# A sixth gate/up product ahead of the router's gate, transposes two products further back, and layer 2's queries copied ahead of weight casts

## What is computed

```python
logits = flat @ router_w.T
scores = jnp.sqrt(jax.nn.softplus(logits))
_, idx = jax.lax.top_k(scores + expert_bias, K)          # K = 4 of E = 32
topv = jnp.take_along_axis(scores, idx, axis=1)
topv = topv / (topv.sum(axis=-1, keepdims=True) + 1e-20)
probs = zeros.at[arange(T)[:, None], idx].set(topv)
def _clamped_swiglu(x, wg, wu, wd):                      # I = 128, ALPHA = 7
    return jax.nn.silu(jnp.clip(x @ wg.T, -ALPHA, ALPHA)) * jnp.clip(x @ wu.T, -ALPHA, ALPHA) @ wd.T
out = sum over the experts of probs[:, e:e+1] * _clamped_swiglu(flat, ...) + _clamped_swiglu(flat, shared ...)
```

## Time and profile before

| | before |
|---|---|
| median of 3 runs | 72.9 us (72.02 to 74.19) |
| profiled execution | 72.22 us |
| its span in the trace | 70.4 us |
| PE busy | 65.3 us, 93% |
| DVE busy | 47.0 us, 67% |
| ACT busy | 46.0 us, 65% |
| POOL busy | 54.2 us, 77% |
| transfers | 15.75 MB, done by about 44 us |
| granted PE clock | full in all slices but the last |

### The profile page before, as it was taken

How to read it: one execution, slowest core, us unless ns; L and a number is a source line. 1 busy time by engine, 2 the same in 40 slices (tenths; PEclk the granted TensorE clock), 3 DMA queues, 4 the chain that set the end, 5 groups by cost and what they waited for, 6 DMA issues and landing times.

```text
span 70.4 us, 1578 instructions
## 1 busy us (share of the span) xinstructions
PE 65.3 (93%) x542; PEld 48.5 (69%) x542; DVE 47.0 (67%) x133; ACT 46.0 (65%) x101; POOL 54.2 (77%) x60
## 2 busy tenths in 40 slices
PE   5999989999799999999989999999999999999940
PEld 2348647789564496467666878888887888788820
DVE  0089488486497536499999945679955887697440
ACT  0606375876998654769979899999668851275220
POOL 7430003889999996998799999999999999999000
PEclk9999999999999999999999999999999999999999
DMA  0998999999999999999999995200000000000002
GB/s 3 271 297 245 329 425 404 291 328 419 417 419 403 393 401 407 396 383 388 393 407 400 391 372 201 76 0 0 0 9 0 0 0 0 0 0 0 0 0 74
DMA packets 6343, 15.75 MB, mean 224 GB/s; under 512 B 704, under 2 KB 1472, under 8 KB 6336
## 3 DMA queue, kind: packets, MB, share of 16 engines
q1 hardware_dynamic: 6048, 15.39, 59.2%
q10 hardware_dynamic: 288, 0.27, 1.1%
HBM read 15.52 MB, written 0.13 MB: 222 GB/s over the span
## 4 chain that ended last, share of the span: by engine, by line
PE 52%; DMA 16%; DVE 14%; SPq 7%; ACT 4%; issue 3%; DVEq 0%; ACTq 0%
DMA gu_raw<-moe_w_dram 16%; PE bP L591 16%; PE bY L624 7%; PE bY L613 6%; PE bXT L603 5%; SPq L275 4%; PE bE L591 4%; DVE gu_clip L964 4%; PE bY L626 3%; SPq L283 2%; DVE h L1018 2%; PE bP L419 2%; PE bXT L448 1%; PE bXT L641 1%; PE bY L444 1%
## 5 line engine op out<-in xcount | busy, mean ns | idle before, releaser
L349 POOL TENSOR_TENSOR gu_w<-gu_raw,gu_w 128x512 fp32r<-128x512 f32 x27 | 33.7, 1277 | 0.6 <-ACT gu_w L705 0.6
L591 PE MATMUL bP<-gu_w,xnT_parts 128*128 128x512 f32 x66 | 18.6, 417 | 0.0
L591 PEld LDWEIGHTS bP<-gu_w,xnT_parts 128*128 128x128 f32 x66 | 12.2, 188 | 2.9 <-issue 0.5
L1018 DVE SCALAR_TENSOR_TENSOR h<-gu_clip,gate,bP 128x128 f32<-128x128 f32 x26 | 7.8, 344 | 5.2 <-ACT bP L790 5.2
L964 DVE TENSOR_SCALAR gu_clip<-bP,clip_at 128x512 f32<-128x512 f32 x13 | 10.4, 806 | 1.1 <-PE bP L591 1.1
L355 POOL TENSOR_TENSOR gu_w<-dn_w,gu_w 128x512 fp32r<-128x512 f32 x8 | 10.1, 1285 | 0.0
L698 ACT ACTIVATE gu_w<-gu_raw 128x1024 fp32r<-128x1024 f32 x9 | 9.4, 1048 | 0.3 <-issue 0.3
L796 ACT ACTIVATE hT_parts<-bXT 128x256 fp32r<-128x256 f32 x11 | 4.2, 383 | 7.1 <-PE bXT L603 7.1
L705 ACT ACTIVATE gu_w<-gu_raw 128x512 fp32r<-128x512 f32 x10 | 6.1, 621 | 1.2 <-DMA gu_raw<-moe_w_dram 1.2
L603 PE MATMUL bXT<-consts_sb,h 128*128 128x128 f32 x33 | 6.5, 277 | 0.3 <-DVE h L1018 0.2
L790 ACT ACTIVATE bP<-gu_clip,rstd 128x256 f32<-128x256 f32 x13 | 6.1, 472 | 0.4 <-DVE gu_clip L964 0.4
(11 more groups left out here) (161 smaller groups left out, 124.8 us busy)
## 6 DMA issues: line engine op xcount, KB each, us to landing
gu_raw<-moe_w_dram SPq DMA_DIRECT2D x16, 512.0 KB, 9.6
dn_w<-moe_w_dram SPq DMA_DIRECT2D x16, 256.0 KB, 9.5
aw_sb<-attn_w_dram SPq DMA_DIRECT2D x2, 512.0 KB, 7.4
shared_sb<-shared_w_dram SPq DMA_DIRECT2D x1, 416.0 KB, 14.9
small_sb<-small_dram SPq DMA_DIRECT2D x1, 338.0 KB, 7.3
xwq_sb<-x_wq_dram SPq DMA_DIRECT2D x1, 256.0 KB, 3.5
lora_sb<-lora_dram SPq DMA_DIRECT2D x1, 256.0 KB, 4.7
ctx_sb<-ctx_kv_dram ACTq DMA_DIRECT2D x1, 192.0 KB, 3.2
```

The lines of the kernel that those rows point to most:

```text
L349: nc.gpsimd.tensor_tensor(gu_w[:, gu_slot(p), 1, cols], gu_raw[:, raw_slot(p), cols], gu_w[:, gu_slot(p), 0, cols], ALU.subtract).then_inc ...
L591: last = nc.tensor.matmul(bGU[n % 5][:, 0:GU], xnT_parts[:, a, k, :], gu_w[:, gu_slot(n - 1), w, k * GU:(k + 1) * GU], start=(k == 0 and a ...
L1018: last = nc.vector.scalar_tensor_tensor(h[:, n % 4, e], gu_clip[:, n % 4, e, 1, :], weight_e, bank[:, e * 2 * I:e * 2 * I + I], ALU.mult, ...
```

## The change

First, `gate_up(6)` gets a bank of its own, `bXT1` (called `bOnce`), and is put ahead of `transpose_h(0)`; `gate_up(7)` stands between transposes 0 and 1. From then on `gate_up(n + 6)` stands ahead of `transpose_h(n)` until the pairs run out at n = 10, where it was `gate_up(n + 4)` until n = 12. `gate_up(n)` now waits for `gate_h(n - 6)` up to n = 11, and for `gate_h(n - 5)` from 12 on, since `bXT1` is used for a product only once. Since `bXT1` is taken, transposes 0 to 6 all go to `bXT0`, and each waits for the reader of the one just before it; from 7 on they alternate again.

The router's scratch values move to `bXT0`. The silu of the shared expert is written into the bank of pair 1, so `silu_unit(0)` waits for `clip(1)` and `gate_h(0)` for `silu_unit(1)`. The copy of `leftover` moves from the end of the router's chain on DVE to a place behind `logits_n`, ahead of a wait for ACT.

Last, ACT copies query 0 ahead of the first half of raw pair 4 and query 1 ahead of its second half, and casts only half of pair 5 ahead of the softmax; the other half follows `copy_probsT(1)`.

The core of the diff:

```diff
+BANKS = 6
+LEADS = ()
+def ahead(n):
+    return min(n + BANKS - sum(n >= at for at in LEADS), PAIRS)
...
-        logits_n, den, inv_root = (bXT1[:, at:at + E] for at in (64, 128, 192))
-        score2, weight = (bXT1[:, at:at + E + 1] for at in (256, 320))
-        bHT = (bXT1, bXT0)
+        logits_n, den, inv_root = (bShared[:, at:at + E] for at in (288, 320, 352))
+        score2, weight = (bShared[:, at:at + E + 1] for at in (384, 448))
-        bGU = (bP[0][:, 0], bP[0][:, 1], bP[1][:, 0], bP[1][:, 1], bE)
+        bOnce = bXT1
+        def bGU(n):
+            if n == BANKS:
+                return bOnce
+            return (bP[0][:, 0], bP[0][:, 1], bP[1][:, 0], bP[1][:, 1], bE)[(n if n < BANKS else n - 1) % 5]
+        def bHT(n):
+            return bXT0 if n <= BANKS or n % 2 == 0 else bXT1
...
             def gate_up(n):
-                if n > 5:
-                    pe.wait_ge(h_ready, n - 4)
+                if n > BANKS:
+                    pe.wait_ge(h_ready, n - BANKS + (1 if n < 2 * BANKS else 2))
...
             def transpose_h(n, width=2):
                 pe.wait_ge(h_ready, n + 1)
-                if n >= 2:
-                    pe.wait_ge(hT_ready, n - 1)
-                if n - 2 > FIRST:
-                    pe.wait_ge(hT_low_ready, n - 2 - FIRST)
+                back = 1 if n <= BANKS else 2
+                if n >= back:
+                    pe.wait_ge(hT_ready, n - back + 1)
+                if n - back > FIRST:
+                    pe.wait_ge(hT_low_ready, n - back - FIRST)
...
-            for n in range(WHOLE + 1, 6):
+            for n in range(WHOLE + 1, BANKS + 1):
                 gate_up(n)
             transpose_h(0, width=1)
+            gate_up(BANKS + 1)
             transpose_h(1)
             for n in range(2, PAIRS + 1):
-                if n + 4 <= PAIRS:
-                    gate_up(n + 4)
+                if ahead(n) > ahead(n - 1):
+                    gate_up(ahead(n))
                 transpose_h(n)
...
             for c in range(DC):
-                gu_high_chunk(WHOLE + 2, c)
                 act.wait_ge(q_psum, DC + c + 1)
                 nc.scalar.activation(qT[:, 1, c], bP[c][:, 1, 0:T], ACT.Identity,
                                      bias=small_sb[:, BIASQ + c:BIASQ + c + 1]).then_inc(q_ready, 1)
-            gu_high(WHOLE + 3)
+                gu_high_chunk(WHOLE + 2, c)
+            gu_high_chunk(WHOLE + 3, 0)
             exp_half(1, 0)
...
             copy_probsT(1)
+            gu_high_chunk(WHOLE + 3, 1)
             gu_high(WHOLE + 4)
...
             def silu_unit(n):
-                act.wait_ge(clip_ready, n + 1)
+                act.wait_ge(clip_ready, max(n, 1) + 1)
...
             step(nc.vector.tensor_scalar(logits_n, bLogits, rstd[:, 2:3], None, ALU.mult))
+            dve.wait_ge(zeroed, 3)
+            step(nc.vector.tensor_copy(score2[:, E:E + 1], leftover[:]))
             dve.wait_ge(one_plus_ready, 1)
...
             step(nc.vector.tensor_tensor(inv_root, inv_root, softplus[:], ALU.mult))
-            dve.wait_ge(zeroed, 3)
-            step(nc.vector.tensor_copy(score2[:, E:E + 1], leftover[:]))
```

More of the change, by code:

```diff
@@ L590, in gate_up @@
                         for a, w in HI_LO:
-                            last = nc.tensor.matmul(bGU[n % 5][:, 0:GU], xnT_parts[:, a, k, :],
+                            last = nc.tensor.matmul(bGU(n)[:, 0:GU], xnT_parts[:, a, k, :],
                                                     gu_w[:, gu_slot(n - 1), w, k * GU:(k + 1) * GU],
@@ L597, in transpose_h @@
                 pe.wait_ge(h_ready, n + 1)
-                if n >= 2:
-                    pe.wait_ge(hT_ready, n - 1)
-                if n - 2 > FIRST:
-                    pe.wait_ge(hT_low_ready, n - 2 - FIRST)
+                back = 1 if n <= BANKS else 2
[3 more added lines that the diff above has]
+                    pe.wait_ge(hT_low_ready, n - back - FIRST)
                 for e in range(width):
-                    last = nc.tensor.transpose(bHT[n % 2][:, e * T:(e + 1) * T], h[:, n % 4, e, :], ident)
+                    last = nc.tensor.transpose(bHT(n)[:, e * T:(e + 1) * T], h[:, n % 4, e, :], ident)
                 last.then_inc(hT_psum, 1)
@@ L619, in down @@
                     if n == PAIRS:
-                        pe.wait_ge(h_ready, PAIRS)
+                        pe.wait_ge(h_ready, PAIRS + 1)
                     for e in range(2):
@@ L785, in silu_unit @@
             def silu_unit(n):
-                act.wait_ge(clip_ready, n + 1)
+                act.wait_ge(clip_ready, max(n, 1) + 1)
                 width = 2 if n else 1
-                bank = bGU[n % 5] if n else bShared
-                dst = bank[:, 0:width * 2 * I].rearrange("p (e w i) -> p e w i", e=width, w=2)[:, :, 0, :]
+                dst = bGU(max(n, 1))[:].rearrange("p (e w i) -> p e w i", e=2, w=2)
+                dst = dst[:, :, 0, :] if n else dst[:, 0:1, 1, :]
                 nc.scalar.activation(dst, gu_clip[:, n % 4, 0:width, 0, :], ACT.Silu, scale=rstd[:, 2:3]
@@ L795, in hT_unit @@
                 dst = hT[:, n % 3, 0:width] if n <= FIRST else hT_parts[:, n % 3, 0]
-                nc.scalar.activation(dst, bHT[n % 2][:, 0:width * T], ACT.Copy).then_inc(hT_ready, 1)
+                nc.scalar.activation(dst, bHT(n)[:, 0:width * T], ACT.Copy).then_inc(hT_ready, 1)
             def dn_high(i):
@@ L821, in _ @@
                 for i in range(UNITS, LAST):
-                    if dn_from(i) + 1 == n + 4:
+                    if ahead(n - 3) <= dn_from(i) < ahead(n - 2):
                         dn_high(i)
@@ L956, in clip @@
                 width = 2 if n else 1
-                bank = bGU[n % 5] if n else bShared
+                bank = bGU(n) if n else bShared
                 if n:
@@ L1010, in gate_h @@
             def gate_h(n):
-                dve.wait_ge(silu_ready, n + 1)
+                dve.wait_ge(silu_ready, max(n, 1) + 1)
                 if n >= 4:
                     dve.wait_ge(hT_psum, n - 3)
-                bank = bGU[n % 5] if n else bShared
+                bank = bGU(max(n, 1))
+                at = 0 if n else I
                 for e in range(2 if n else 1):
@@ L1018, in gate_h @@
                     last = nc.vector.scalar_tensor_tensor(h[:, n % 4, e], gu_clip[:, n % 4, e, 1, :], weight_e,
-                                                          bank[:, e * 2 * I:e * 2 * I + I], ALU.mult, ALU.mult)
+                                                          bank[:, at + e * 2 * I:at + e * 2 * I + I], ALU.mult, ALU.mult)
                 last.then_inc(h_ready, 1)
@@ L1030, in hT_low @@
                 dve.wait_ge(hT_ready, n + 1)
-                nc.vector.tensor_tensor(hT_parts[:, n % 3, 1], bHT[n % 2][:, 0:2 * T].rearrange("p (e t) -> p e t", e=2),
+                nc.vector.tensor_tensor(hT_parts[:, n % 3, 1], bHT(n)[:, 0:2 * T].rearrange("p (e t) -> p e t", e=2),
                                         hT_parts[:, n % 3, 0], ALU.subtract).then_inc(hT_low_ready, 1)
```

2 lines of the change are left out of this document (1 added, 1 removed).

## The result

The changed kernel took 73.6 us in the median of five runs (72.65 to 74.65), the kernel before 72.47 us in five (71.79 to 74.19). The ratio is 1.0134, with the interval 1.0082 to 1.0186: between 0.8 and 1.9% slower. The forecast was 0.6% faster by ratio (0.994), and 72.1 us with a range of 71.1 to 73.3, so the measured median lies outside it. A later comparison of the same two kernels, with 12 and 35 runs, gave 1.0034 (0.9988 to 1.008), which can't be told from no change. Ratios leave disturbed executions out, medians hold all of them.

What follows compares the result with a forecast made beforehand. PE, busy 93% of the span, was taken as the bound, so only its waits could go: 0.36 (queries) + 0.95 (gate) - 0.89 (tail) = 0.42 us saved, 71.80 on the profiled execution; forecast 72.1 us, range 71.1 to 73.3.

Steps and rivals of the forecast that it cites:

- The queries' 0.36 us: Layer 2's first scores: PE no longer waits for the query copy behind a cast on ACT; 0.36 us saved, bounds 0 to 0.36.
- The tail's loss: Transposes 13 and 14: PE waits for DVE's work on the last pairs; 0.89 us lost, bounds 0 to 1.9.
- the queries' 0.36 is lost: Rival: one gain fails, by a cast late for POOL, heads copied late, or first transposes waiting; 72.2 us, 13%.
- The gate: Between product 5 and transpose 2: products 6 and 7 moved forward end PE's standing still; 0.95 us saved, bounds 0.6 to 0.95.
- The scratch bank, the silus and the copy of `leftover`: Smaller edits around the router, gate and transposes 0 to 6: expected to change nothing unless ACT falls a whole step behind.
- product 16 never waited for POOL: Expected sign: POOL ends the last low part at 55.07, product 16 starts at about 57.0; no cost.
- DVE's steps that don't overlap: Rival in the tail: each DVE step costs 1.83 us instead of 1.57; 0.56 us slower, 72.78 us, 9%.
- The rival on the other side: The rival of DVE steps without overlap in the tail: 1.83 us each, 0.56 us slower in all, 9%.

Runs made afterwards that it cites:

- The gate's half alone: The changed kernel with layer 2's new order of query copies and casts undone, against the kernel before: ratio 1.0074 (1.0025 to 1.0122).
- LEADS = (7, 9): The changed kernel with no product put ahead of transposes 7 and 9, against the kernel before: ratio 0.9935 (0.989 to 0.9981).

## Why the prediction was wrong

Two terms of the sum failed. The queries' 0.36 us were counted whole, and the runs show about nothing in most executions, 0.15 at the middle over three pairs of kernels. The tail's loss was put at 0.89 us and measured 1.22. Of the 0.78 us between the forecast (0.42 saved) and the profiles without the query's wait (0.36 lost), these two make 0.69.

**The queries.** The failed step is "I take the whole 0.36". The wait was in the profile, the mechanism was right, and the changed kernel's scores have no wait. But what ended the wait was a query copy behind a cast that itself had waited 0.71 us for a transfer, and that part is there in few executions. Of five profiles with the old order of ACT one shows the whole wait, one 0.11 us, and three none, two of these with a late start of layer 2. Measured by itself the edit gave 1.0009 (0.9965 to 1.0053). The rival "the queries' 0.36 is lost" was there, with 13%, but for the wrong reasons: I looked for a new wait that takes the gain, not for whether the old wait is there in most executions. ACT's copy of the heads came as counted, at 24.56 with no idle time ahead of it, and cost nothing.

**The gate.** Right within a tenth: 0.95 counted, 0.86 found. The kernel with the queries' edit alone has its S at 17.18 and transpose 9 at 54.99; with the gate's edit as well S is at 17.21 and transpose 9 at 56.98, with two more products ahead of it. That is 54.99 + 2.82 + 0.03 - 56.98 = 0.86. The sum's 0.95 was reached by a slip: it went on from the start of transpose 0's row (35.10) with slot lengths and compared the result with a slot. Product 5's row, in the timeline of the kernel before, ends at 35.23:

```profile
33.67 1.56 PE L591 MATMUL bP<-gu_w,xnT_parts 128*128 128x512 f32 x6
```

From there the slots (0.11, 0.22, 1.41) lead to 36.97, which leaves 0.82 to transpose 2's slot at 37.79. The scratch bank, the silus and the copy of `leftover` cost nothing that the trace shows, and product 16 never waited for POOL.

**The tail.** The mechanism is right to the row: pair 12's hidden values 2.08 us behind transpose 9 (56.98, 59.06), steps of 1.57 us on DVE (59.06, 60.63, 62.20, 63.77), and waits for low parts ahead of transposes 13 and 14. Its size was not: 0.89 us counted, 1.22 lost. From transpose 9 to the end of down 15 the kernel with the queries' edit alone needs 67.29 - 54.99 - 2.82 = 9.48 us, the changed one 67.68 - 56.98 = 10.70. From transpose 9 to transpose 14 it took 7.01 us against 6.00 of PE work (54.99 + 2.82 to 63.81 in the kernel with the queries' edit alone), so transpose 14 was 1.01 us late and not 0.89: PE started 0.13 us after the low part's end (63.86, 63.99), where I had put 0.04, and the rest is the count of PE's work, 6.03. And from there to the end it took 3.69 instead of 3.48 us, since a pair of transposes that PE had to wait for holds its slot for 0.41 us and not 0.22, and all behind is 0.19 later. This term had no place in the sum, by the same slip as at the gate: 63.01 is when transpose 14's row can start, and it was compared with 62.12, a slot. In an unbroken sequence a slot begins 0.17 us behind the row's start (transpose 9: row 56.81, slot 56.98). Counted alike on both sides, 63.01 + 0.41 - 0.22 - 62.12 = 1.08 us would have been lost in the tail and 0.82 won at the gate, and the sum without the queries would already have been 0.26 us slower.

**DVE's steps that don't overlap.** This rival, that of the Trainium skill's rule (VectorE: DVE Perf Modes, section The DRAIN you can't avoid), is refuted for these shapes: by it a step would be 1.83 us, and the changed kernel's rows are 1.57 apart even where the queue is full. The same section adds that an instruction that is not held starts earlier, and the rows agree with that part.

**The sum.** Without the queries' part it is 0.95 - 0.89 = 0.06 us saved in the forecast, and 0.86 - 1.22 = 0.36 us lost in the trace, which is 50.47 - 50.11, the D - S of the changed kernel less that of the kernel with the queries' edit alone. Against executions of the kernel before that have no wait for the query, the change costs 0.36 of about 72.5 us, a ratio of 1.005. The gate's half alone measured 1.0074 (1.0025 to 1.0122), the whole 1.0034 (0.9988 to 1.008): both agree with it. The first comparison, 1.0134 (1.0082 to 1.0186), does not. In its profiled pair the rest is the head, 0.87 us, where both kernels issue the same instructions; that the head also set its other runs is likely but not shown, since only profiled executions can be split. The rival on the other side was put at 0.56 us slower with 9%, by a mechanism that isn't there. That the gains could be smaller and the loss larger by a few tenths each had no place in the rivals, though the whole saving of 0.42 us was a difference between terms of about one.

**The forecast for the better version.** By the trace the order with `LEADS = (7, 9)` saves 0.8 us on an execution without the query's wait (50.11 - 49.30), 1.1%; measured are 0.65% (0.2 to 1.1), at the edge of the interval. Late transfers, as in its variant with 12 warm-up products, may take some of it in other executions. That wasn't measured.

## What to carry to other kernels

A wait that ends with a transfer's landing belongs to the execution that was profiled: before its price enters a sum, follow it back, and count it whole only if several executions show it. Row starts and slots must not be mixed in one sum: here they lie 0.17 us apart at full pace, and two such slips hid 0.32 us of a forecast gain of 0.42. When products are moved ahead, count for every engine the work that must now fit between the last of them and the end; a lead that hides a late start has to be given back before the end, and where it is given back needs the same count on the engines behind. A difference of a few tenths between two terms of one microsecond is not a forecast of the sign, and each wait that is added costs more than the idle time of its row.

## What the runs showed of the chip

**The start of TensorE's higher clock moves between executions, and costs as much as the whole change.** Nine identical products of 512 columns from 0.76 us on took 3.38, 3.45, 3.48, 3.54, 3.62, 3.74, 3.84 and four times 4.00 us in eleven profiles. At 4.00 they are all at the lower level (0.43 us each), and the context's four products behind them took 1.01 to 1.22 us instead of 0.71. The row of the granted clock on the page has full speed there in every slice, so it can't be used to see this; the durations can. The Trainium skill (TensorE: Matmul & The Clock Gate, section Part 1: The HAM clock gate) says that this penalty varies from run to run and puts it at under 1% of a typical span. The traces agree on the first; on the second, the 0.87 us at S between two profiles here are 1.2% of the time.

**A transfer's landing moves between executions too.** Raw pair 4 (512 KB, issued at the same place of the queue) landed between 16.00 and 18.38 us in twelve profiles. The next pair landed 1.27 to 1.29 us behind it in every one of them.

**A wait of TensorE costs more than the idle time of its row.** A pair of 128x128 transposes holds 0.22 us where PE comes to it at full pace, and 0.41 us in each of the four waits in the tails above: 0.19 us beside the idle time that the row shows. Most of it is overlap that is lost and not slower work: at full pace the pair's row starts about 0.17 us before the row ahead of it ends. From start to start transposes 14 and 15 of the changed kernel are 0.96 us apart (63.99, 64.95), where 11 and 12 are 0.93 apart (60.06, 60.99).
